# Layer 0 of a four-layer graph network: the first linear product by seven half-size products per pair of tiles, from the third group on

## The reference, cut to what matters

```python
def hypergraph_conv(x, adj, W, b):
    H = (adj != 0); w = adj.reshape(N, -1)[:, :C]
    xw = x @ W.T
    Dn = 1 / (H @ w); Be = 1 / H.sum(axis=1)
    m = Be[:, :, None] * (H.T @ xw)
    return Dn[:, :, None] * (H @ m) + b
h = relu(hypergraph_conv(h0, adj, W1, b1))   # W1: 512 -> 1024
h = layer_norm(h, gamma, beta)               # over 1024
y = hypergraph_conv(h, adj, W2, b2)          # W2: 1024 -> 512
x = x + y + h0                               # h0 = relu(layernorm(x))
```

## Time and profile before

| | us |
|---|---|
| median of 3 runs | 2630.46 (2630.12 to 2632.95) |
| the profiled execution | 2627.68 |
| its span in the trace | 2625.9 |
| busy: PE, DVE, POOL, ACT | 2591.7, 1843.3, 1472.8, 1406.1 |
| granted TensorE clock | 0.999 of full speed |

### The profile page before, as it was taken

How to read it: one execution, slowest core, us unless ns; L and a number is a source line. 1 busy time by engine, 2 the same in 40 slices (tenths; PEclk the granted TensorE clock), 3 DMA queues, 4 the chain that set the end, 5 groups by cost and what they waited for, 6 DMA issues and landing times.

```text
span 2625.9 us, 44958 instructions
## 1 busy us (share of the span) xinstructions
PE 2591.7 (99%) x12938; PEld 2173.1 (83%) x12938; DVE 1843.3 (70%) x4093; ACT 1406.1 (54%) x2623; POOL 1472.8 (56%) x2283
## 2 busy tenths in 40 slices
PE   7999999999999999999999999999999999999999
PEld 6888888888888888888888888888888887788887
DVE  8877777777777766666666666666667676677776
ACT  5443444434444555454545455666566665666665
POOL 6544454444444654333333335777777767877776
PEclk9999999999999999999999999999999999999999
DMA  3111111111111321111111112222222223444443
GB/s 117 55 47 40 38 42 38 42 44 38 35 41 38 98 85 51 52 50 52 50 52 50 52 50 87 84 93 76 98 76 96 78 80 118 134 140 152 151 136 120
DMA packets 145389, 195.25 MB, mean 74 GB/s; under 512 B 55475, under 2 KB 55475, under 8 KB 145334
## 3 DMA queue, kind: packets, MB, share of 16 engines
q1 hardware_dynamic: 138560, 183.55, 21.4%
q10 hardware_dynamic: 6774, 11.03, 1.3%
HBM read 127.42 MB, written 67.11 MB: 74 GB/s over the span
## 4 chain that ended last, share of the span: by engine, by line
PE 93%; DVE 2%; POOL 2%; issue 1%; ACT 1%; DMA 0%; ACTq 0%; POOLq 0%; DVEq 0%
PE ps L584 27%; PE ps L586 27%; PE ps L585 26%; PE ps L601 6%; PE ps L626 4%; PE ps L604 2%; POOL w_lo L1476 1%; DVE row_lo L1122 0%; ACT row_hi L842 0%; POOL row_lo L1476 0%; PE ps L765 0%; PE ps L772 0%; DMA raw<-w_t 0%; POOL x_res L1589 0%; DVE stats L1216 0%
## 5 line engine op out<-in xcount | busy, mean ns | idle before, releaser
L584 PE MATMUL ps<-w_hi,col_hi 128*128 128x512 f32 x2432 | 970.0, 399 | 4.9 <-DVE w_lo L1122 3.8
L586 PE MATMUL ps<-w_hi,col_lo 128*128 128x512 f32 x2432 | 950.3, 391 | 0.0
L585 PE MATMUL ps<-w_lo,col_hi 128*128 128x512 f32 x2432 | 948.4, 390 | 0.0
L584 PEld LDWEIGHTS ps<-w_hi,col_hi 128*128 128x128 f32 x2432 | 457.6, 188 | 98.4 <-issue 7.9
L586 PEld LDWEIGHTS ps<-w_hi,col_lo 128*128 128x128 f32 x2432 | 457.0, 188 | 98.9
L585 PEld LDWEIGHTS ps<-w_lo,col_hi 128*128 128x128 f32 x2432 | 458.4, 188 | 87.5
L842 ACT ACTIVATE col_hi<-ps 128x512 fp32r<-128x512 f32 (+1 forms) x512 | 291.1, 578 | 225.3 <-PE ps L604 116.0
L1500 POOL TENSOR_TENSOR var_eps<-moments,eps_ln 128x1 f32<-128x1 f32 x256 | 51.2, 200 | 481.0 <-DVE moments L1139 480.8
L1476 POOL TENSOR_TENSOR row_lo<-normed,row_hi 128x512 fp32r<-128x512 f32 x160 | 207.4, 1297 | 197.2 <-ACT row_hi L842 195.3
L601 PE MATMUL ps<-adj_both,row_hi 128*128 128x256 f32 x1024 | 246.6, 329 | 0.2 <-DVE deg L1177 0.2
L1126 DVE TENSOR_TENSOR wide<-ps,col_hi 128x512 f32<-128x512 f32 x256 | 175.5, 686 | 78.7 <-ACT col_hi L842 76.1
(11 more groups left out here) (181 smaller groups left out, 4798.6 us busy)
## 6 DMA issues: line engine op xcount, KB each, us to landing
out<-x_res SPq DMA_DIRECT2D x256, 256.0 KB, 2.0
...
x_res<-out SPq DMA_DIRECT2D x128, 256.0 KB, 3.2
...
```

The source lines that it names most:

```text
L584: nc.tensor.matmul(out_ap, lhs_hi, rhs_hi, start=start, stop=False, **checks)
L585: nc.tensor.matmul(out_ap, lhs_hi, rhs_lo, start=False, stop=False, **checks)
L586: return nc.tensor.matmul(out_ap, lhs_lo, rhs_hi, start=False, stop=stop, **checks)
```

## The change

**The product.** Groups 0 and 1 keep `lin1` (their steps are now in `order_hyper` and the new `order_turn`). From group 2 on, `lin1` of two tiles a, b (pair u = 0, 1) is done by seven products of 128 rows by 256 by 512, 6 matmuls each: 42 instead of 48. Four of them take sums of quarters of the mixed rows (`sums0` on DVE, four operations of 256 columns that read `wide` and write `wide`; `sumsplit0` on ACT and POOL), and four take differences of quarters of W1, which are made once. Three partial results are copied out of PSUM with the degree as scale (`q1`, `p6`, `s5` on ACT), the other four are added onto them or the bias (`c11`, `c22`, `c12`, `c21` on DVE), and POOL adds the bias to three (`b11`, `b22`, `b12`). `adj0` is now gathered in full precision in `wide` first, and `adj0c` (ACT, POOL) splits it into `col_hi`, `col_lo`.

**The weights.** The eight blocks of differences are loaded, made and split in groups 0 and 1 (`load_seven`, `make_seven`, `stage_seven`); the loads and sums for layer 2's score vectors move from group 1 to group 2, which is now written out too.

**The bank.** `hyp` writes bank 1; it waits for `rowb_lo` of its slot (DVE has read the second linear product) instead of `final`, and `adj0` waits for `final`.

**The orders.** In groups 2 to 14 each of the four engines has its own list (`ENGINE_ORDERS`); group 15 has a new shared one. Layers 1 to 3 keep theirs.

```diff
@@ PE
+            def sevenths(g, name, u):
+                a, b = 2 * u, 2 * u + 1
...
+                if name == "p1":
+                    pe.wait_ge(s0["adj0_lo"], n(g, a))
+                    last = seventh(0, (a, 1), col_hi[:, a, 0:2 * P], col_lo[:, a, 0:2 * P], "B11")
...
+                if name == "p6":
+                    wait_pair0(pe, "copied", "p1", g, u)
+                    pe.wait_ge(sp2["sum_lo"], 2 * np0(g, u) - 1)
+                    last = seventh(0, (a, 1), sum0_hi[:, 1, :], sum0_lo[:, 1, :], "T2", start=False)
...
                 if name == "hyp":
                     pe.wait_ge(s0["binc"], i)
                     if not first(g):
-                        pe.wait_ge(s["final"], i - SLOTS)
-                    nc.tensor.matmul(ps[:, t, 0, 0:P + 2], inc_t[:, t, :], binc_w[:, t, :], start=True, stop=False)
+                        pe.wait_ge(s0["rowb_lo"], i - SLOTS)
+                    nc.tensor.matmul(ps[:, t, 1, 0:P + 2], inc_t[:, t, :], binc_w[:, t, :], start=True, stop=False)
...
                 if name == "adj0":
                     pe.wait_ge(s0["d_sum"], i)
+                    if not first(g):
+                        pe.wait_ge(s["final"], i - SLOTS)
@@ ACT
+                if name == "sumsplit0":
...
+                    wait_pair0(act, "sums", "s2", g, u)
+                    copy(sum0_hi[:, 0:2, :], quarters_of(wide[:, 2 * u, F:HID])).then_inc(sp2["sum_hi"], 1)
+                    wait_pair0(act, "sums", "s4", g, u)
+                    copy(sum0_hi[:, 2:4, :], quarters_of(wide[:, 2 * u + 1, F:HID])).then_inc(sp2["sum_hi"], 1)
+                if name == "q1":
+                    wait_pair0(act, "products", "p1", g, t)
+                    wait_pair0(act, "sums", "s4", g, t)
+                    act.wait_ge(s0["degree"], 5 * g + 5)
+                    scale_copy(wide[:, 2 * t, 0:F], ps[:, 2 * t, 1, :], deg[:, D_OUT, 2 * t:2 * t + 1]).then_inc(sp2["copied"], 1)
@@ DVE
+                if name == "sums0":
...
+                    V.tensor_tensor(sum0_full(u, 0), bottom[:, 1, :], bottom[:, 0, :], ALU.add).then_inc(sp2["sums"], 1)
+                    V.tensor_tensor(sum0_full(u, 2), top[:, 0, :], bottom[:, 0, :], ALU.subtract)
+                    wait_pair0(dve, "sums", "s1", g, u)
+                    V.tensor_tensor(sum0_full(u, 1), sum0_full(u, 0), top[:, 0, :], ALU.subtract).then_inc(sp2["sums"], 1)
+                    wait_pair0(dve, "sums", "s2", g, u)
+                    V.tensor_tensor(sum0_full(u, 3), top[:, 1, :], sum0_full(u, 1), ALU.subtract).then_inc(sp2["sums"], 1)
@@ POOL
+                if name == "adj0c":
+                    pool.wait_ge(s0["adj0_hi"], i)
+                    lo_of(col_lo[:, t, own0(t)], wide[:, t, own0(t)], col_hi[:, t, own0(t)]).then_inc(s0["adj0_lo"], 1)
+                if name in ("b11", "b22", "b12"):
...
+                    Q.tensor_tensor(at, at, b0a_bc[:, half, :], ALU.add).then_inc(s0["biased"], 1)
@@ the ends of the new lists, groups 2 to 14
+    ("PE", 0, "mid"): [
+        ("adj0", 3), ("p6", 0), ("p5", 0), ("p7", 0), ("p3", 0), ("p4", 0), ("p1", 1), ("p2", 1), ("p6", 1),
...
+        ("adj0_n", 1), ("hyp_n", 2), ("adjb", 2), ("linb", 3), ("adj0_n", 2), ("adjb", 3), ("hyp_n", 3),
+        ("p1_n", 0), ("p2_n", 0),
+    ("ACT", 0, "mid"): [
...
+        ("split_n", 2), ("hyp_n", 2), ("sumsplit0_n", 0), ("linb", 3), ("adj0c_n", 1), ("norm_n", 3),
+        ("adj0_n", 2), ("split_n", 3), ("hyp_n", 3), ("adj0c_n", 2), ("q1_n", 0),
+    ("DVE", 0, "mid"): [
...
+        ("adj0hi_n", 0), ("trb", 3), ("adj0hi_n", 1), ("sums0_n", 0), ("hyp_n", 2), ("adjb", 2), ("linb", 3),
+        ("adj0hi_n", 2), ("adjb", 3), ("hyp_n", 3), ("deg_n", 0),
+    ("POOL", 0, "mid"): [
+        ("resid", 0), ("resid", 1), ("b11", 0), ("b22", 0), ("b12", 0), ("sumsplit0", 1), ("adj0c", 3), ("mid", 0),
...
+        ("adj0c_n", 0), ("split_n", 2), ("sumsplit0_n", 0), ("adj0c_n", 1), ("split_n", 3), ("adj0c_n", 2),
```

More of the change, by code:

```diff
@@ L99, in last_hyper @@
     return [
[L100 to L109, removed]
[6 rows of a table added]
+        ("p4", 1), ("tra", 1), ("relu0", 2), ("relu0", 3), ("mid", 3), ("stats_n", 1), ("trb", 0), ("norm_n", 0),
+        ("midnorm", 2), ("residb", 2), ("lina", 0), ("midnorm", 3), ("lina", 1), ("tra", 2), ("stats_n", 2),
+        ("trb", 1), ("stats_n", 3), ("linb", 0), ("trb", 2), ("tra", 3), ("split_n", 0), ("lina", 2),
+        ("asplit_n", 0), ("linb", 1), ("residb", 3), ("adjb", 0), ("norm_n", 1), ("linb", 2), ("trb", 3),
+        ("lina", 3), ("adj0_n", 0), ("asplit_n", 1), ("split_n", 1), ("norm_n", 2), ("asplit_n", 2), ("adjb", 1),
+        ("split_n", 2), ("bias0_n", 0), ("adjb", 2), ("adj0hi_n", 0), ("linb", 3), ("adj0hi_n", 1), ("norm_n", 3),
+        ("adj0_n", 1), ("asplit_n", 3), ("adj0_n", 2), ("bias0_n", 1), ("bias0_n", 2), ("split_n", 3),
+        ("adj0hi_n", 2), ("adjb", 3),
     ]
@@ L478, in wait_operand, with order_of @@
         def wait_operand(eng, layer, op):
[L480 removed]
+            eng.wait_ge(sw["lo"], STEPS.index((layer, op, 3 if op == "W0" else 1)) + 1 + len(SEVEN_OPS))
         block = ctx.enter_context(nc.Block())
+        def order_of(engine, layer, order):
+            return ENGINE_ORDERS.get((engine, layer, "mid"), order) if order is ORDERS[layer] else order
         def groups(eng, layer, body):
[L486 to L488 removed]
+            unrolled = 3 if layer == 0 else 2
+            for g in range(unrolled):
+                body(layer, g, FIRST_ORDERS[g] if layer == 0 and g < 2 else ORDERS[layer])
+            with eng.Fori(unrolled, GROUPS - 1) as g:
                 body(layer, g, ORDERS[layer])
@@ L794, in _ @@
             SEVEN = ("tr", "p1", "p2", "p6", "p5", "p7", "p3", "p4")
-            WORK = [(hyper, ("hyp", "adj0", "lin1", "tra", "lina", "trb", "linb", "adjb")),
+            WORK = [(hyper, ("hyp", "adj0", "lin1", "p1", "p2", "p6", "p5", "p7", "p3", "p4", "tra", "lina", "trb", "linb", "adjb")),
                     (gcn, ("adj0", "adj1", "adj2", "lin0", "lin1", "lin2")),
@@ L1051, in body @@
             def body(layer, g, order):
+                order = order_of("ACT", layer, order)
                 last = isinstance(g, int) and g == GROUPS - 1 and layer == 0
@@ L1388, in body @@
             def body(layer, g, order):
+                order = order_of("DVE", layer, order)
                 for place, (name, t) in enumerate(order):
@@ L1604, in body @@
             def body(layer, g, order):
+                order = order_of("POOL", layer, order)
                 last = isinstance(g, int) and g == GROUPS - 1 and layer == 0
```

317 lines of the change are left out of this document (264 added, 53 removed), and 18 rows, old and new, of the table LEAK.

## The result

The changed kernel takes 2688.69 us in the median of 4 runs (2685.55 to 2694.10), the kernel before 2630.29 in 4 (2628.12 to 2632.95). The ratio is 1.0224, 95% interval 1.0202 to 1.0245: 58 us slower. I had said 2665, in a range of 2597 to 2682: slower, as it came out, but 24 us too little, and above the range. The profiled execution after took 2694.1 us with a span of 2692.3, at a mean granted clock of 0.986, where before had 0.999.

What follows compares the result with a forecast made beforehand. PE's matmuls were taken to bound the kernel. Per group 55.53 - 2.72 - 0.45 + 3.0 + 2.4 + 0.3 = 58.1 us, 35 us more in 14 groups, so a median of 2665 us, range 2597 to 2682.

Steps and rivals of the forecast that it cites:

- the sum: Looped group: 55.53 less matmuls and old waits, plus new waits, gives 58.1 us, 2.5 more; 35 us in 14 groups.
- The products: `lin1` on PE: 12 fewer matmuls per group at 0.227 us, 2.72 us less, 38.1 us in 14 groups.
- The degrees: Ahead of `p6` 0: PE waits for the `deg` chain and `q1`, 2.4 us a group (1.5 to 2.9).
- The sums: Loop's end: DVE sums take turns with POOL, so PE waits at `adj0_n` 2 or `adjb` 3, 3.0 us a group.
- The upper bound: Loop's end, the four DVE sums taking turns with POOL: PE waits some 3.3 us a group.
- The price of 0.79: DVE load: each 256-column sum priced at 0.79 us, the middle value of the nearest earlier row, L1310.
- The rest of the body: After `p4` 0 the longest chain needs some 8.5 us against PE's 9.5; 0.3 us a group allowed.
- The 0.45 that I took for the bank: Loop's end: PE's two waits of the kernel before, at `adjb` 3 and `hyp` 3, go; 0.45 us a group less.
- What I put at nothing: W1 differences in groups 0 and 1, moved score sums, new unrolled group, queues: no cost, at most some 3 us once.
- A: Rival: the waits at sums and degrees do not come; 53.3 us a group, about 2599 (2592 to 2608); chance 0.27.
- B: Rival: only the degrees' wait comes, not the sums'; 55.7 us a group, about 2633 (2620 to 2640); chance 0.25.
- D: Rival: DVE or POOL falls behind in the middle of the group too; above 2682 us; chance 0.05.

Runs made afterwards that it cites:

- e4: Changed kernel plus twelve 512-column matmuls that nothing reads, ahead of `p6` 0 in a free bank: 2681.33 us.
- e10: Changed kernel with all work kept, engine lists remade and first and last groups' order mended: 2628.00 us, ratio 0.9993 to before.
- e11: As e10, with the last group's `resid` 0 and 1 moved again and `trb` 3 ahead of `adj0_n` 0: 2625.74 us.
- e6: Kernel before with only the bank change (`hyp` in bank 1 and the waits that go with it): 2623.95 us, ratio 0.9974.
- e1: Changed kernel with POOL's `resid` of slots 0 and 1 on 32 of 512 columns in the seven-product groups: 2650.20 us.
- e8: Changed kernel with POOL's `resid` 0 and 1 and low parts of `adj0c_n` 0 and `split_n` 2 on 32 columns: 2621.56 us.

## Why the prediction fell short

**The step that failed** is the sum: "Per group: 55.53 - 2.72 - 0.45 ... + 3.0 + 2.4 + 0.3 = 58.1". It prices a wait of PE by its own length. Nothing in it stands for the granted clock, which I had read as 0.999 throughout and taken as given. Behind these waits it falls to the lower level, and by the table this costs 32.1 us in the 13 groups of that stretch, 2.5 in each. With it the sum reads, by what was measured: 55.5 - 2.7 - 0.45 + 2.34 + 2.47 + 2.5 = 59.7, against 59.6. That the fall comes from the waits, and not from the new matmuls, e4 shows: with the same products and PE kept busy ahead of `p6` 0 the loss is 11.1; and with all of them and few long waits (e10, e11) it is 1.6.

My sum for the profiled execution was 2663, and it took 2694.1. That these 31 us are close to the 32 of the clock is in part chance: my terms for the sums and for the rest were too high by 0.9 us a group, and groups 0 to 2 cost more than I gave them. By PE's rows the last matmul of `adjb` 3 in group 2 starts at 192.21 before and at 207.84 after, with two `adj0` more done (1.8 us): 13.8 us later, where I had 2.5. The twelve looped groups add 3.9 each, where I had 2.5, and the rest of the program 5.7, where I had 2.5. So of the 31 us 11 lie in groups 0 to 2, 17 in the loop and 3 behind it. (The median lies 5.4 below the profiled execution, so against it I was 24 low.)

**The products**: right. The page has 168 matmuls less. That their time comes off at least in part is seen where little waits: in e11 the group takes 53.92 us, and in e6, with the same bank and the old products, 54.99.

**"The degrees"**: right in place and size. I took 2.4 us; it is 32.1 in 13 times, 2.47. The first `deg` operation starts at 387.10 and the last that `q1` needs ends at 391.54, 4.4 us where I had 3.93, and e1 shows the cause. With `resid` out of the way e1 has 5.7 us in 13 groups, 0.4 each.

**"The sums"**: right in mechanism, too high in size. I took 3.0 (2.4 to 3.3); it is 30.4 in 13, 2.34. Of the four sums two took turns, as these rows of after show, and two found POOL idle:

```profile
379.02 1.42 DVE L1456 TENSOR_TENSOR wide<-wide 128x256 f32<-128x256 f32 x1
380.36 1.50 DVE L1457 TENSOR_TENSOR wide<-wide 128x256 f32<-128x256 f32 x1
381.79 0.41 DVE L1459 TENSOR_TENSOR wide<-wide 128x256 f32<-128x256 f32 x1
382.23 0.42 DVE L1461 TENSOR_TENSOR wide<-wide 128x256 f32<-128x256 f32 x1
```

The upper bound took a third turn, which needs an operation on POOL that waits itself for the copy of the sums. The price of 0.79 that I took for a sum from the earlier trace rows fits: over ten groups the 80 sums take 58.8 us, 0.74 each.

**"The rest of the body"**: 0.3 allowed, nothing of it seen: from 190 to 960 us the list has 1.5 us beside the two large waits and 0.7 of issue. The 0.45 that I took for the bank was 0.52 by e6.

**What I put at nothing** was not nothing. I had looked at groups 0 and 1, and together they come 3.4 us later (the last matmul of `adjb` 3 in group 1 starts at 141.45 instead of 137.17, with one `adj0` more done), with a wait of 2.0 us at 140.87: under the 5 us that I had named as a sign of being wrong. But group 2, the first with seven products, costs another 10.4, where a looped one costs 3.9: its first `p6` 0 waits 5.0 us (151.77), twice what I had given the degrees, and the clock is at the lower level around that wait. Layers 1 to 3 are as they were: `lin2` of layer 1 starts 64.5 us later, the span is 66.4 longer.

**The rivals.** A needed that the waits don't come; e8 takes away what makes them and has 2622. Some 15 of the 23 us up to it from 2599 lie in groups 0 to 2, where the last matmul of `adjb` 3 starts at 207.26: 13.2 us later than before by the same count, where A has 2.2 less. Some 8 lie in the loop, 53.93 a group where A has 53.3. A part of that is a price that I didn't know: a wait costs PE more than the idle time that the view shows. An idle time is counted from the modelled end of the last matmul, and in an unbroken run the next one starts 0.16 us before that end (0.39 against 0.227); and the first matmul behind a wait is followed after 0.33 us instead of 0.23. In e10:

```profile
484.07 0.39 PE L736 MATMUL ps<-w_hi,w_lo 128*128 128x512 f32 x1
484.81 0.49 PE L734 MATMUL ps<-w_hi,col_hi 128*128 128x512 f32 x1 [0.35 <-DVE wide L1469]
485.14 0.40 PE L735 MATMUL ps<-w_lo,col_hi 128*128 128x512 f32 x1
```

From 484.07 to 484.81 are 0.74 us where 0.227 are due, with 0.35 shown as idle: 0.16 more, and 0.1 behind it, so about 0.25 by this estimate. The windows of ten loop bodies each, of e6, e10 and after, say about the same (length, PE busy, clock):

```profile
281.57:831.46 549.89, 548.91 (x2761) 1.00 0.13 41
287.41:831.58 544.17, 530.83 (x2642) 1.00 0.13 41
302.04:898.10 596.06, 548.92 (x2653) 0.96 0.12 37
```

From e6's 548.91 go 27.2 for 120 matmuls, which leaves 521.7. e10 has 9.1 more and four waits in a body, 0.23 each. After has 27.2 more; 23 to 24 of them are the clock, and the other 3 or 4 are 0.15 to 0.2 for each of its 20 waits. For a wait of 0.35 us this price is most of what it costs, for one of 3 us it is small. It was worked out from rows and not tested by a run of its own. B is out, since the sums bite as well. D did not come: no wait in the middle of a looped group.
